# Second step's up projection ahead of the first routing weights, three more dummy matmuls, and the second pair's statistics, h and logits one step later

## The reference

```python
x = x + _wkv(w, u, _layernorm(x), ctx)          # a recurrence over the 64 tokens
h = _layernorm(x)
probs = softmax(h @ gate_w)                     # 32 experts
w, sel = top_k(probs, 8); w = w / sum(w)
# each expert takes at most C = 2 * (1024 * 8 // 32) tokens, in token order
x = x + sum over chosen experts e of  w_e * (silu(h @ w_gate[e]) * (h @ w_up[e])) @ w_down[e]
```

## Time and profile before

| | |
|---|---|
| median of 3 runs | 252.53 us (252.33 to 253.0) |
| profiled execution | 253.08 us, of which span 251.3 us |
| mean granted PE clock | 0.992 |
| busy PE | 238.8 us (95%) |
| busy PEld | 200.8 us (80%) |
| busy DVE, ACT, POOL | 138.6, 133.0, 152.1 us |
| chain that ended last | PE 76%, DVE 10%, issue 6%, DMA 3% |

### The profile page before, as it was taken

The page is one execution under the profiler, slowest core; times in us unless marked ns, Lnnn a source line. Parts: engine busy times, 40 slices in busy tenths (PEclk is TensorE's granted clock), DMA queues, the critical chain, the costliest instruction groups (busy, mean ns, idle before and its releaser), DMA issues.

```text
span 251.3 us, 4352 instructions
## 1 busy us (share of the span) xinstructions
PE 238.8 (95%) x1410; PEld 200.8 (80%) x1410; DVE 138.6 (55%) x357; ACT 133.0 (53%) x248; POOL 152.1 (61%) x143
## 2 busy tenths in 40 slices
PE   5777999999999999999999999999999999999993
PEld 2433989998888878889878889888888888888883
DVE  4589875994579647973885482332324242424233
ACT  2797558554894477558736623353535343434411
POOL 6137842357966794687686224486868686768620
PEclk9999799999999999999999999999999999999999
DMA  6951661000605233060505100004142323500002
GB/s 180 273 160 41 167 181 52 3 3 3 172 16 133 79 92 98 20 188 13 175 6 148 41 3 0 0 3 127 63 116 76 101 87 82 186 6 0 3 0 85
DMA packets 38414, 19.97 MB, mean 79 GB/s; under 512 B 29944, under 2 KB 38392, under 8 KB 38392
## 3 DMA queue, kind: packets, MB, share of 16 engines
q1 hardware_dynamic: 37544, 19.27, 26.8%
q10 hardware_dynamic: 848, 0.43, 0.7%
HBM read 18.65 MB, written 1.05 MB: 78 GB/s over the span
## 4 chain that ended last, share of the span: by engine, by line
PE 76%; DVE 10%; issue 6%; DMA 3%; POOL 2%; ACT 1%; ACTq 1%; DVEq 0%; POOLq 0%
PE bank L825 47%; PE bank L865 23%; DMA ctx_sb<-in_ctx_dram 3%; DVE state L1069 2%; POOL t_lo L434 2%; DVE bank L1093 2%; PE bank L846 1%; DVE t_sb L1275 1%; DVE t_sb L1269 1%; PE bank L702 1%; PE bank L766 1%; PE bank L742 1%; POOL wlo L403 1%; DVE inv L1111 1%; DVE stats L1025 1%
## 5 line engine op out<-in xcount | busy, mean ns | idle before, releaser
L434 POOL TENSOR_TENSOR t_lo<-t_sb,t_hi 128x512 fp32r<-128x512 f32 (+1 forms) x53 | 62.0, 1169 | 70.1 <-ACT t_hi L631 66.7
L825 PE MATMUL bank<-h_hi,whi 128*128 128x512 f32 (+1 forms) x216 | 85.1, 394 | 0.4 <-DVE t_sb L1275 0.2
L403 POOL TENSOR_TENSOR wlo<-raw,whi 128x768 fp32r<-128x768 f32 x42 | 77.4, 1845 | 6.7 <-ACT whi L594 6.2
L825 PE MATMUL bank<-h_hi,wlo 128*128 128x512 f32 (+1 forms) x216 | 80.6, 373 | 0.0
L825 PE MATMUL bank<-h_lo,whi 128*128 128x512 f32 (+1 forms) x216 | 80.5, 373 | 0.0
L631 ACT ACTIVATE t_hi<-t_sb 128x512 fp32r<-128x512 f32 (+1 forms) x54 | 31.5, 584 | 81.7 <-DVE t_sb L1275 81.6
L1269 DVE TENSOR_TENSOR t_sb<-bank,s_sb 128x512 f32<-128x512 f32 (+1 forms) x54 | 34.0, 629 | 70.6 <-ACT s_sb L624 36.2
L865 PE MATMUL bank<-whi,t_hi 128*128 128x256 f32 x192 | 49.7, 291 | 0.1
L865 PE MATMUL bank<-wlo,t_hi 128*128 128x256 f32 x192 | 48.1, 282 | 0.0
L825 PEld LDWEIGHTS bank<-h_hi,wlo 128*128 128x128 f32 x216 | 41.4, 192 | 7.6
L825 PEld LDWEIGHTS bank<-h_hi,whi 128*128 128x128 f32 x216 | 41.7, 193 | 5.7 <-DVE t_sb L1275 0.4
(11 more groups left out here) (131 smaller groups left out, 183.9 us busy)
## 6 DMA issues: line engine op xcount, KB each, us to landing
raw<-in_L_ffn_w_gate_dram SPq DMA_DIRECT2D x14, 384.0 KB
raw<-in_L_ffn_w_up_dram SPq DMA_DIRECT2D x14, 384.0 KB
raw<-in_L_ffn_w_down_dram SPq DMA_DIRECT2D x42, 128.0 KB
out_dram<-x SPq DMA_DIRECT2D x4, 256.0 KB, 2.5
x_sb<-in_x_dram SPq DMA_DIRECT2D x1, 512.0 KB, 7.7
ctx_tile<-in_ctx_dram SPq DMA_DIRECT2D x4, 128.0 KB, 6.2
x_sb<-in_x_dram SPq DMA_DIRECT2D x1, 256.0 KB, 3.5
ctx_sb<-in_ctx_dram SPq DMA_DIRECT2D x1, 256.0 KB, 6.0
```

What stands on the lines that cost most here:

```text
L403: pool.tensor_tensor(split_view(wlo, slot, part), raw_parts(slot, part), split_view(whi, slot, part).bitcast(F32), ALU.subtract).then_inc( ...
L434: pool.tensor_tensor(t_lo[k % 2][:, c], t_sb[:, c], t_hi[k % 2][:, c].bitcast(F32), ALU.subtract).then_inc(t_lo_ready, 1)
L825: last = nc.tensor.matmul(ps[:, c], up_weight(w, slot, part, k, j), h[:, k, tokens], start=(i == 0), stop=(i == len(terms) - 1))
```

## The change

On PE: one more dummy behind the first pair's `turn_h` (three instead of two) and two dummies inside `logits` of the first pair, between the products with the high part of h and the wait for the low part. The up projection of step 1 is issued ahead of the first turn, so ahead of the routing weights of step 0. `turn_h(second)` moves from the end of step 2 to the middle of step 3, `logits(second)` and `turn_kv(third)` from step 3 to step 4. On DVE: `stats_h(second)` moves from step 0 to step 1, `h_low(second)` from step 2 to step 3, `largest(second)` from step 3 to step 4, ahead of `choose`. On POOL: `power(second)` moves from step 0 to step 1. ACT's order isn't changed, nor is any DMA.

```diff
--- before.py
+++ after.py
@@ -449,7 +449,7 @@
                             split_low(ahead % 2, k % GT, pair_before(half, it) * 2 + ahead, steps_of_last_user(half, it, ahead))
 
             third = later(2)
-            turn(0, 0, PASSES, {(0, 0): [lambda: power(second, second.second_norm)],
+            turn(0, 0, PASSES, {(0, 1): [lambda: power(second, second.second_norm)],
                                 (0, 2): [lambda: power(third, third.first_norm)]}, split=(2,))
             def tiles_beside(it, k):
                 at, back, _, front = cycle(it, k)
@@ -771,6 +771,7 @@
                     for t in range(u.tiles):
                         for k in range(KT):
                             with_hi(t, k, start=False, stop=False)
+                    keep_clock(2)
                 pe.wait_ge(h_lo_ready, u.n + 1)
                 for t in range(u.tiles):
                     if u is not first_routed:
@@ -892,8 +893,9 @@
                     for k in range(TURN_STEPS):
                         n = steps_before(half, it) + (p or 0) * TURN_STEPS + k
                         slot, j = k // GT, k % GT
+
                         started = half == 0 and first_turn and p == 0 and k == 0
-                        if not started:
+                        if not (half == 0 and first_turn and p == 0 and k < 2):
                             project(n, half, p, 1, slot, j, group + slot)
                         if tiles:
                             tiles[0](it, k)
@@ -951,20 +953,21 @@
             pe.wait_ge(rstd_ready, first.second_norm + 1)
             keep_clock(3)
             turn_h(first)
-            keep_clock(2)
+            keep_clock(3)
             logits(first_routed)
             project(0, 0, 0, 0, 0, 0, 0)
             project(0, 0, 0, 1, 0, 0, 0)
             project(1, 0, 0, 0, 0, 1, 0)
+            project(1, 0, 0, 1, 0, 1, 0)
 
             third = later(2)
             turn(0, 0, PASSES, {(0, 0): [lambda: turn_mixed(second)],
-                                (0, 3): [lambda: logits(second_routed), lambda: turn_kv(third)],
+                                (0, 3): [lambda: turn_h(second)],
+                                (0, 4): [lambda: logits(second_routed), lambda: turn_kv(third)],
                                 (1, 0): [first_counts],
                                 (1, 1): [lambda: turn_parts(first_routed)],
                                 (1, 3): [lambda: turn_parts(second_routed)],
-                                (1, 5): [lambda: turn_mixed(third)]},
-                 {(0, 2): [lambda: turn_h(second)]})
+                                (1, 5): [lambda: turn_mixed(third)]})
             def tiles_within(it, k):
                 at, _, routed, _ = cycle(it, k)
                 if at == 2:
@@ -1299,11 +1302,11 @@
                 add_output(0, q)
 
             third = later(2)
-            turn(0, 0, PASSES, {(0, 0): [(add_mixed, second), (stats_h, second)],
-                                (0, 1): [(keep_chosen, first_routed)],
-                                (0, 2): [(stats_x, third), (h_low, second)],
-                                (0, 3): [(largest, second_routed)],
-                                (0, 4): [(choose, second_routed), (keep_chosen, second_routed)],
+            turn(0, 0, PASSES, {(0, 0): [(add_mixed, second)],
+                                (0, 1): [(stats_h, second), (keep_chosen, first_routed)],
+                                (0, 2): [(stats_x, third)],
+                                (0, 3): [(h_low, second)],
+                                (0, 4): [(largest, second_routed), (choose, second_routed), (keep_chosen, second_routed)],
                                 (0, 5): [(weigh, first_routed)],
                                 (1, 0): [(count_first, None), (all_sums, third)],
                                 (1, 1): [(weigh, second_routed)],
```

## The result

| | before | after |
|---|---|---|
| median | 252.69 us (252.33 to 253.0, 6 runs) | 254.22 us (253.92 to 254.53, 6 runs) |
| profiled execution | 253.08 us, span 251.3 | 254.34 us, span 252.6 |
| mean granted PE clock of it | 0.992 | 0.997 |

The ratio is 1.0057 with an interval of 1.0044 to 1.0071: slower by 1.5 us, where 1.4 was forecast.

What follows compares the result with a forecast made beforehand. PE was taken as the bound. Logits 2.4 us later, 1.0 of it hidden by the table load, gave +1.4: 252.53 + 1.4 = 253.9 us, own range 253.4 to 254.3, overall 252.2 to 255.0.

Steps and rivals of the forecast that it cites:

- The bound: PE bounds the kernel; any shift at the matmuls of step 7 (44.54 us) carries to the end one for one.
- The dummies: Three dummies in PE's idle gaps before 25.2 us: cost 0 (0 to 0.1); holding the clock gains 0.2 at best.
- The up projection: Step 1's up projection ahead of step 0's weights: cost 0 at full clock, weights at 28.8 as before.
- The statistics: On DVE, statistics a step later: t_sb 1 1.2 us earlier, var 1.0 later, offset at 34.35.
- ACT: Unchanged ACT queue: norm_h waits for offset, widen ends at 35.85, PE waits 1.35 us before step 3's weights.
- The logits: Logits start 2.4 us later, maximum at 41.2; 1.0 hidden by the table load, so route_exps shifts 1.4 us.
- The hidden delay: Rival: PE doesn't wait for widen, route_exps starts with the table load as before; 252.6 us, chance 0.21.
- the gain: Rival: PE's own work is the only bound between 28.8 and 44.5 us; -0.9 us, 251.6, chance 0.13.
- The falling clock: Rival: clock still falls at 25.2 us, step 0's weights start 0.72 later; +2.1, 254.6 us, chance 0.24.
- The table load: ACT's next activation follows the load's start by 1.30 us; the skill's 2.66 with drain would give 0.8 shift, 253.3.

Runs made afterwards that it cites:

- dummies_only: The kernel before with the three added dummies alone; -0.27 us against the kernel before, ratio 0.9985.
- front_only: The kernel before plus the three dummies and the moved up projection of step 1, second pair's work left in place; -0.02 us against the kernel before.
- widen_first: The changed kernel with widen of the first pair swapped ahead of norm_h of the second on ACT; +0.13 us against the kernel before.
- norm_behind: The changed kernel with norm_h of the second pair moved behind the high copy of step 2 on ACT; +0.56 us against the kernel before.
- later_only: The kernel before with only the second pair's statistics, h and logits (and turn_kv) a step later, PE front unchanged; +1.35 us against the kernel before.
- no_dummies: The changed kernel without its three added dummies; +1.90 us against the kernel before, ratio 1.0075.
- logits_only: The kernel before with only the second pair's logits, the third tile's transposes and largest moved from step 3 to 4; +0.82 us against the kernel before.
- stats_only: The kernel before with only the second pair's statistics and POOL's power moved from step 0 to 1; +0.46 us against the kernel before.

## Why the prediction was right

**The bound.** Right: the shift at the matmuls of step 7 was +1.52 in the trace and +1.53 in the medians; nothing was absorbed behind it.

**The dummies.** Two parts. That they cost nothing held. That the clock is worth nothing in the kernel before was a step mis-sized: the term stood at 0 and dummies_only measures -0.27. The mechanism named, that PE only stands for DVE's wide instead, is what its profile shows. That the clock would hold was no result of the working: no row could show it, the forecast took it at 0.42 against 0.24, and it came out that way.

**The up projection.** Put at 0. In the changed kernel the weights start at 28.65 + 0.27 = 28.92, 0.15 us behind the 28.77 of before; against the full clock it costs a little more: it is held by silu 0 and its six matmuls push the weights to 5.54 us behind L770 in front_only, from 5.32 in dummies_only. That is 0.2 us in the trace. The 0.25 between their medians (-0.02 and -0.27) goes the same way, but their intervals overlap, so it isn't proof. I had set it against the 28.77 of the half clock.

**The statistics.** t_sb 1 was forecast at 31.9 and came at 31.78 + 0.27 = 32.05. The times below have the same 0.27 added, with the forecast in brackets: offset 34.47 (34.35), weights of step 3 at 36.13 (35.9), so no part of the 1.0 us won at t_sb 1 was left, PE's wait 1.21 (1.35).

**ACT.** The centre of the argument. norm_h stood for offset 1.72 us, widen behind it, PE behind widen. widen_first and norm_behind show that it is a cause: nothing but ACT's order is changed in them and 1.4 and 1.0 us come back by the medians (1.0 and 0.85 in the traces).

**The logits.** Logits at 39.74 (39.55), maximum 41.29 (41.2), exponentials at 41.33 released by it, t_sb 5 at 46.01 (45.9). What the sum didn't say is what each move costs by itself: 0.82 for the logits' place and 0.46 for the statistics'. With both made, most of the loss hangs on a third thing, the unchanged place of norm_h on ACT.

**The rivals.** The hidden delay and the gain did not come. The hidden delay was said to need the statistics a microsecond earlier; widen_first takes PE's wait away by another road, and its logits' delay is hidden in part: the exponentials wait 0.29 us for the maximum. The falling clock is not one case against another but a matter of executions. Twelve profiles show how to count them: where the mean granted clock is 0.997 or more (ten) the stretch around 25 us ran at 1.00, where it is 0.992 or 0.993 (two) at about half. Without the dummies 40 of 109 timed executions (the kernel before, later_only, no_dummies, logits_only, stats_only) kept a mean granted clock of 0.996 or more; with them (the changed kernel and six others) 69 of 72 did. Its price in this kernel was put at 0.7, and the trace has 0.58. In no_dummies the one execution at full clock took 253.96 us and the five at lower clock 254.91 in the median, 0.95 more, but one execution is little to go by. In the kernel before, where the wait for wide covers most of it, the medians of the two kinds lie 0.2 to 0.4 us apart (252.59 and 252.82 of 33, 252.72 and 253.0 of 19, 252.62 and 253.0 of 23). The Trainium skill (TensorE: Matmul & The Clock Gate, Part 1) says that the gate's window isn't tied to the start of the kernel. The runs agree with it, though they don't show the cause: one kernel, both outcomes.

**The table load.** In the changed kernel the silu table's load is issued at 42.88 and the activation behind it starts at 44.17, 1.29 us later, as the 1.30 of the earlier trace rows. The drain that the Trainium skill adds (ScalarE: Activation LUTs, "What ACT_TABLE_LOAD costs") is in neither, and the shift was 1.5, not the 0.8 that it gave.

## What to carry to other kernels

When a stage is moved later on one engine, walk the queues of the engines that weren't touched: here ScalarE kept waiting for the moved statistics in its old place, with another unit's work and the main chain queued behind that wait. Before filling an idle piece of the busiest engine, look at what it waits for next; work done early there ends in the next wait, and if the work is itself held by something, it delays what was on time. The chain of a side computation (statistics, normalisation, logits, exponentials, table load) can be the real schedule for a stretch of steps in which the busy engine looks like the bound.

## What the runs showed of the hardware that was not expected

The same kernel runs the stretch ahead of its steps at half clock in most executions and at full clock in others, as read from the mean granted clock: 22 of 75 executions of the kernel before kept 0.996. With three dummy matmuls of 512 columns, some 0.6 us of work in two gaps, 69 of 72 did. The closest comparison is on one chip: 12 of 12 in dummies_only, 11 of 33 in the kernel before. The share without dummies isn't a constant either: with the same front logits_only kept it in 5 of 10 and stats_only in 9 of 12. One profile shows only one of the two.
